# A dense graph attention on one core: where the source's slope term is added

## What is computed

```python
# feature: (3125, 64); src, dst: (100000,)
e = leaky_relu(feature[src] @ a_src + feature[dst] @ a_dst, negative_slope=0.01)
ex = exp(e - segment_max(e, dst)[dst])
hm = segment_sum(ex[:, None] * feature[src], dst) / segment_sum(ex, dst)
h = relu(concatenate([feature, hm], axis=1) @ lin_w.T + lin_b)
```

## Time and profile before

| | us |
|---|---|
| Median of three runs | 4694.56 |
| The profiled execution, its own time | 4687.18 |
| Its span, first to last instruction | 4685.4 |
| Attention phase, its scores ready to the end | 4379 to 4685.4 |
| of which the 25 chunks, first to last `neg` | 4394.7 to 4623.1 |

### The profile page before, as it was taken

How to read it: one execution, slowest core, us unless ns; L and a number is a source line. 1 busy time by engine, 2 the same in 40 slices (tenths; PEclk the granted TensorE clock), 3 DMA queues, 4 the chain that set the end, 5 groups by cost and what they waited for, 6 DMA issues and landing times. The chain is left out here.

```text
span 4685.4 us, 59450 instructions
## 1 busy us (share of the span) xinstructions
PE 2968.8 (63%) x19382; PEld 2193.7 (47%) x19382; DVE 3034.2 (65%) x4651; ACT 1274.4 (27%) x1892; POOL 1881.9 (40%) x1835
## 2 busy tenths in 40 slices
PE   1055556566642477779799699515766667673676
PEld 1034444344421254546556466315665666663455
DVE  9466676667623488756556466446677767774796
ACT  0011111111110277535345245101111111110484
POOL 4577777677762121100000000067777677642000
PEclk9966666666665699989899899657878788876698
DMA  5156666555630488534234144044454554541342
GB/s 178 33 136 152 155 154 150 145 149 149 153 83 13 184 333 325 202 132 157 77 144 160 60 152 149 1 91 86 100 120 100 106 118 93 114 85 26 111 167 73
DMA packets 738112, 599.57 MB, mean 128 GB/s; under 512 B 486055, under 2 KB 676612, under 8 KB 714476
## 3 DMA queue, kind: packets, MB, share of 16 engines
q1 hardware_dynamic: 462650, 389.91, 28.4%
q0 software_dynamic: 64032, 141.68, 10.5%
q10 hardware_dynamic: 211282, 66.03, 6.0%
HBM read 396.80 MB, written 200.61 MB: 128 GB/s over the span
## 5 line engine op out<-in xcount | busy, mean ns | idle before, releaser
L486 POOL DMA_INDIRECT ms_got_s<-table_src,ms_st_src x800 | 845.7, 1057 | 339.8 <-issue 332.1
L1553 POOL DMA_INDIRECT sh_got_s<-sheaf_src,sh_st_src x800 | 783.9, 980 | 301.9 <-issue 239.2
L1728 PE MATMUL sh_pin<-ident,sh_term 128*128 128x128 f32 x3200 | 465.5, 317 | 129.0 <-DVE sh_run L1663 114.5
L1728 PEld LDWEIGHTS sh_pin<-ident,sh_term 128*128 128x128 f32 x3200 | 455.8, 232 | 135.1 <-DVE sh_run L1663 120.2
L1047 DVE CUSTOM_DVE_ANT_0 c_xs<-c_pa,c_logs 128x1024 f32<-128x1024 f32 (+1 forms) x400 | 379.0, 967 | 187.9 <-PE c_pa L1154 109.5
L126 POOL DMA_INDIRECT spread<-dst_tab,first_idx x25 | 24.3, 971 | 1133.1 <-DVEq L100 1125.8
L991 PE MATMUL c_pa<-c_esT,c_v 128*64 128x128 f32 (+1 forms) x5000 | 399.8, 286 | 86.2 <-DVE c_esT L1061 61.7
L991 PEld LDWEIGHTS c_pa<-c_esT,c_v 128*64 128x64 f32 (+1 forms) x5000 | 278.0, 138 | 224.7 <-issue 119.3
L973 PE MATMUL c_pa<-ident,c_xs 128*128 128x128 f32 x2500 | 370.3, 287 | 0.0
L1154 PE MATMUL c_pa<-c_kT,c_q_st 64*128 64x512 f32 (+1 forms) x800 | 340.7, 546 | 43.4 <-DVE c_peaks L1047 27.7
L614 PEld LDWEIGHTS ms_pc<-ms_hot_l,ms_hot_x 128*125 128x125 bf16 x1408 | 211.5, 208 | 283.6 <-issue 263.5
(11 more groups left out here) (368 smaller groups left out, 5193.4 us busy)
## 6 DMA issues: line engine op xcount, KB each, us to landing
c_logs<-logs SPq DMA_DIRECT2D x75, 1562.5 KB, 6.5
prefix<-ms_sums SPq DMA_DIRECT2D x44, 1792.0 KB
logs<-c_logs SPq DMA_DIRECT2D x25, 1562.5 KB, 8.0
at_logs<-logs SPq DMA_DIRECT2D x25, 1562.5 KB
runs<-ms_out_t ACTq DMA_DIRECT2D x200, 128.0 KB
sh_cont<-cont SPq DMA_DIRECT2D x100, 256.0 KB
sums<-sh_out_t ACTq DMA_DIRECT2D x100, 256.0 KB
ms_seq<-in_dst_seq SPq DMA_DIRECT2D x200, 64.1 KB
```

What stands on the lines that cost most here:

```text
L486: pool.indirect_dma_start(got_s[u][:, i, q, :], None, dram["table_src"], bass.IndirectOffsetOnAxis(st_src[u][:, i, q:q + 1].bitcast(U32), ...
L1553: pool.indirect_dma_start(got_s[r][:, 4 * i + k, :], None, dram["sheaf_src"], bass.IndirectOffsetOnAxis(st_src[u][:, i, k:k + 1].bitcast(U ...
L1728: ins = pe.matmul(pin[j % 2][:, P * (i % 4):P * (i % 4) + P], term[:, 4 * i + 2 * k:4 * i + 2 * k + 2, :].rearrange("p t f -> p (t f)"), k ...
```

## The change

The source's slope term no longer goes into `xs` but into the loaded logarithms. GpSimd, in a block of its own, waits for each chunk's load and adds `src_low` to the 128 x 3125 tile in place, one instruction for each chunk; the first peak step of a chunk waits for that (semaphores `slopes_in`), not for the load. The factor 0.99 moves into ScalarE's relu as its scale, with `col` scaled beforehand. That relu is now cut into the four pieces of the peak steps, which wait for it directly, and VectorE's `prepare` is gone.

```diff
+        self.logs_ready = self.logs_in
...
-                dve.wait_ge(self.logs_in[i % self.buffers], n_in)
+                dve.wait_ge(self.logs_ready[i % self.buffers], n_in)
...
+        sm.logs_ready = [ph.sem(f"slopes_in{k}") for k in range(sm.buffers)]
...
+        @block.gpsimd
+        def _(pool):
+            pool.wait_ge(low_made, 1)
+            for c in range(NC):
+                k = c % sm.buffers
+                logs = sm.logs[k][:, 0:N]
+                pool.wait_ge(sm.logs_in[k], 16 * (c // sm.buffers + 1))
+                pool.tensor_tensor(logs, logs, src_low[:, :], ALU.add).then_inc(sm.logs_ready[k], 16)
...
-            def prepare(c, i, b):
-                xs = sm.xs[i % 4]
-                lo, m = PAIRS[b]
-                dve.wait_ge(relued, c * 2 + (2 if lo + m > HALVES[0][1] else 1))
-                dve.scalar_tensor_tensor(xs[:, lo:lo + m], xs[:, lo:lo + m], 1.0 - SLOPE, src_low[:, lo:lo + m],
-                                         ALU.mult, ALU.add).then_inc(scored, 1)
...
                 for b in range(NS):
                     if more:
-                        prepare(c + 2, i + 2, b)
+                        peak(c + 2, i + 2, b)
                     if b < 3:
                         sm.vector_odd(dve, c, 2 * b + 1)
-                    if more and b:
-                        peak(c + 2, i + 2, b - 1)
                 if more:
-                    peak(c + 2, i + 2, NS - 1)
                     sm.vector_neg(dve, c + 2, i + 2)
                 sm.vector_out(dve, c, i)
...
-            def relu(c, i, h):
-                lo, hi = HALVES[h]
-                act.activation(sm.xs[i % 4][:, lo:hi], src_all[:, lo:hi], ACT.Relu,
-                               bias=col[:, ds(c, 1)] if type(c) is not int else col[:, c:c + 1]).then_inc(relued, 1)
+            def relu(c, i, b):
+                lo, m = PAIRS[b]
+                act.activation(sm.xs[i % 4][:, lo:lo + m], src_all[:, lo:lo + m], ACT.Relu, scale=1.0 - SLOPE,
+                               bias=col[:, ds(c, 1)] if type(c) is not int else col[:, c:c + 1]).then_inc(scored, 1)
```

More of the change, by code:

```diff
@@ L1899, in attention_phase @@
         sm.dv = ph.sem("peak_steps")
+        sm.logs_ready = [ph.sem(f"slopes_in{k}") for k in range(sm.buffers)]
         v, pa, flat = sm.v, sm.pa, sm.flat
-        (loaded, turned, copied, mm, low_made, relued, scored, dv, joined, back, normed, done) = (ph.sem(n) for n in (
-            "loaded", "turned", "copied", "mm", "low_made", "relued", "scored", "dv", "joined", "back", "normed", "done"))
+        (loaded, turned, copied, mm, low_made, scored, dv, joined, back, normed, done) = (ph.sem(n) for n in (
+            "loaded", "turned", "copied", "mm", "low_made", "scored", "dv", "joined", "back", "normed", "done"))
         block = ph.block()
@@ L1964, in _ @@
             dve.wait_ge(mm, 1)
-            dve.tensor_copy(col[:, 0:NC], pa[:, 7, 0:NC])
+            dve.tensor_scalar(col[:, 0:NC], pa[:, 7, 0:NC], 1.0 - SLOPE, None, ALU.mult)
             dve.tensor_copy(src_all[:, :], flat[:, 0:NP]).then_inc(copied, 1)
@@ L1980, in _ @@
             for c in range(2):
-                for b in range(NS):
-                    prepare(c, c, b)
                 for b in range(NS):
@@ L2020, in _ @@
             act.activation(src_low[:, :], flat[:, 0:N], ACT.Copy, scale=SLOPE).then_inc(low_made, 1)
-            def relu(c, i, h):
-                lo, hi = HALVES[h]
-                act.activation(sm.xs[i % 4][:, lo:hi], src_all[:, lo:hi], ACT.Relu,
-                               bias=col[:, ds(c, 1)] if type(c) is not int else col[:, c:c + 1]).then_inc(relued, 1)
+            def relu(c, i, b):
+                lo, m = PAIRS[b]
+                act.activation(sm.xs[i % 4][:, lo:lo + m], src_all[:, lo:lo + m], ACT.Relu, scale=1.0 - SLOPE,
+                               bias=col[:, ds(c, 1)] if type(c) is not int else col[:, c:c + 1]).then_inc(scored, 1)
             for c in range(3):
-                for h in range(2):
-                    relu(c, c, h)
+                for b in range(NS):
+                    relu(c, c, b)
             for h in range(2):
@@ L2040, in body @@
                     relu(c + 3, i + 3, 0)
+                    relu(c + 3, i + 3, 1)
                 sm.scalar_even(act, c, 6)
@@ L2044, in body @@
                 if sm.has(c + 3):
-                    relu(c + 3, i + 3, 1)
+                    relu(c + 3, i + 3, 2)
+                    relu(c + 3, i + 3, 3)
             sm.loop(act, body)
```

## The result

The changed kernel takes 4798.23 us (median of four runs, 4791.0 to 4809.33), the kernel before 4695.58 us: a ratio of 1.0221, interval 1.0200 to 1.0241. The forecast was 4779 us, slower. The profiled execution took 4799.12 us, its span is 4797.3 us.

What follows compares the result with a forecast made beforehand. The prediction took VectorE to bound the chunk loop at 9.52 us a chunk. With 23 chunks of 13.1 us, the last `neg` came +84.4 us later: 4687.2 became 4771.6, plus 7.4 for the median, 4779 us; range 4722 to 4830.

Steps and rivals of the forecast that it cites:

- The bound before: Chunk loop of the kernel before: VectorE bounds it at 9.52 us a chunk, TensorE and ScalarE having slack.
- ScalarE's pace: Chunk loop without a collision and with a short enough ring: ScalarE sets 8.5 to 8.6 us a chunk; chance 0.06.
- VectorE's 3.5 us: Chunk loop: prepares of three times 1024 and one of 53 columns leave VectorE, 3.5 us a chunk.
- The exclusion: Attention peak steps: VectorE with two SBUF inputs and GpSimd's add block each other for the whole instruction; chance 0.79.
- the gather that "keeps its 0.94 us": Profile row: a GpSimd gather beside a peak step reading PSUM and one SBUF tile, read as not held back.
- The pattern: Chunk loop: load lands, add holds the small last peak, next load waits behind that peak; 13.1 us a chunk.
- the other pattern of the prediction: Chunk loop: small peak slips in first, two adds back to back, then two chunks' peaks; 12.25 us a chunk.
- L: Time from a chunk's last peak step to its buffer's next load having landed, with the semaphore: 6.1 us.
- A: GpSimd's add of one chunk, with fixed part and hand-over to the waiting engine: 6.5 us.
- R: What VectorE has left of a chunk's peaks after the add: 0.5 us, between 0.2 and 2 us.
- the sum: Whole kernel: 23 chunks of 13.1 us after the start, last `neg` +84.4 us; forecast 4779 us.
- L + A as the law: Chunk loop: load and add in series though there are two buffers, 6.1 + 6.5 + 0.5 = 13.1 us a chunk.

## Why the prediction was right

- **The bound before, and what goes.** The loop without the add runs at 8.63 us; the prediction had 8.5 to 8.6 for ScalarE's pace. The two extra relu pieces were put at 0.5 us a chunk, and two pieces less gave 0.4 back. VectorE's 3.5 us can't be read off, since it no longer bounds; its busy time fell from 9.2 to 6.2 us a chunk.
- **The exclusion** was taken from GpSimd's gathers held by VectorE; that it also works the other way for a whole instruction was marked as taken by likeness. The add beside the kernel before shows it. One of the prediction's rows carries less than was read from it: the gather that "keeps its 0.94 us" beside a peak step from PSUM started first and shares only its last 0.2 us with it; the run with 75 adds in those layers is the evidence for that side. The gathers held by VectorE also seemed to say that a writing instruction is held; the memset shows no such thing in the loop. So the gather probably is held by something it does at its start, such as reading its index column. The kernel before has rows for this: a gather from 1698.09 to 1699.51 is past its start when VectorE's add of two SBUF tiles begins at 1698.97, and that add takes its usual 3.42 us. No run tests it. The Trainium skill (SBUF — State Buffer, Who interferes with whom) states the rule, two SBUF inputs against a GpSimd instruction that reads; the runs agree on every side of it that they touch.
- **The pattern.** Small last peak held, load behind it, then the next add: as described, in most periods. Twice in the loop, and at its start, two adds come back to back (13.5 us together), the other pattern of the prediction; there two chunks take about 27.3 us, 13.6 each and not 12.25. Of the 2.8 us more, 0.9 are the load, 0.5 the two adds, and the rest is the stretch from the adds' end to the small peak, 6.9 us in place of 5.4, with TensorE late.
- **The size.** The pace from the second `neg` on is 14.0 us, forecast 13.1; that is 20.7 of the 21.6 us by which loop and start came out longer, the start has 0.9. The terms: L is 7.0, not 6.1, because I ended it with the traffic and 0.2 us, while the waiting engine starts some 0.8 us behind the last traffic. A is 6.8, not 6.5: a little more per column than was put together from the memset and the affine select; the Trainium skill's 4497 ns for 2048 columns (GPSIMD Engine Reference, Elementwise — side-by-side cycle accounting) gave an estimate of 6.9, nearer. R is 0.1, not 0.5: the add starts while VectorE is in the copy ahead of the small peak. Nor did R grow to 2 us as the clock fell, as the prediction feared, because the wait for TensorE and that copy lie beside the load and the add. The three make some 0.7 us more a chunk, and the adds do follow each other at 13.8 us (22 steps from 4413.27 to 4717.57); the remaining 4 us lie at the loop's two ends. That the median missed by only 19 us has some luck in it: the profiled execution was taken 7.4 us under its median before and 0.9 us above it after, and measured from one profiled execution to the other the sum missed by 27.5.
- **L + A as the law.** The prediction put load and add in series because of two buffers. With four buffers the adds follow at 13.6 us all the same, and with four buffers and the add started at the last peak, where GpSimd waits for no load, at 13.7. So that reason was wrong while the number was right, and that 7.0 + 6.8 comes so near to them is luck. What counts is where the add starts relative to VectorE's two-input work: the body's own length, 7.7 us here with TensorE partly at half clock, plus what of the add is not hidden, 6.2. The run started at the third peak differs from the one at the last peak in nothing else, and its pace is 1 us shorter.
- **What stayed open.** How much of the 7.7 us is the clock. It is 0.74 in the loop against 0.98, and four transposes that took 0.66 us at full clock take 1.12 at 4578.17; but no run held the clock up with the add in place.

## What to carry to other kernels

Work with SBUF inputs moved from VectorE to GpSimd is no relief where the VectorE work that stays has two SBUF inputs: look at the inputs of what stays, then count the moved instruction's length less what VectorE would have idled. If it must be there, cut it into pieces, start it where VectorE waits or works from PSUM, and only then deepen the ring. Best is to look for algebra that takes the term out of the loop.

## What the runs showed of the hardware

- An instruction that is held shows as a long one: 53 columns took 5.6 to 6.5 us, and its idle time before is 0.0: the mean ns tells, not the waits.
- A GpSimd add of 3125 columns takes 6.82 us from two tiles, 5.40 us when both inputs are the same tile, a memset of the same size 2.71 us.
- VectorE's copies from PSUM ran unchanged, 0.69 us, beside the add. Its copy of 1600 columns from SBUF to SBUF, 0.98 us long alone, took 1.63 us beside a GpSimd memset.
